# Taking four second counts of ScalarE ahead of all exponentials of a place, in a macaron attention block

## The reference

```python
q, k, v = (hidden @ W.T split into 32, 8 and 8 heads of 32)     # Wq, Wk, Wv
k, v = repeated 4 times over the heads
qr, kr = apply_rope(q, cos, sin), apply_rope(k, cos, sin)
draft = einsum('bhqd,bhkd->bhqk', qr, kr) + causal_mask
num_remain = max(min(S, 128), S - int(S * 0.9))                 # 205 of 2048
_, idx = top_k(draft, num_remain)
mask = 0 at idx, the lowest float elsewhere; the future is masked too
attn = softmax(draft_scores / sqrt(32) + mask)
out = (attn @ v) @ Wo.T
```

## Time and profile before

| | us |
|---|---|
| median of three runs | 4355.48 |
| the profiled execution, its own time | 4352.74 |
| span of its profile | 4351.0 |
| TensorE matmul busy | 3364.8 |
| VectorE busy | 3187.2 |
| ScalarE busy | 2688.8 |
| GpSimd busy | 1989.4 |

### The profile page before, as it was taken

One profiled execution on the slowest core, in us unless ns is written; L12 is line 12 of the kernel. 1 busy time (PEld: TensorE's weight loads), 2 busy tenths in 40 slices (PEclk: granted clock), 3 DMA queues, 4 the chain that ended last, 5 costly groups with the idle time before them and its releaser, 6 DMA issues. The chain is left out here.

```text
span 4351.0 us, 55631 instructions
## 1 busy us (share of the span) xinstructions
PE 3364.8 (77%) x15624; PEld 1559.5 (36%) x15864; DVE 3187.2 (73%) x6121; ACT 2688.8 (62%) x4577; POOL 1989.4 (46%) x5916
## 2 busy tenths in 40 slices
PE   7999936886787567887875678988657888886997
PEld 3444412332333233333332233333323333433444
DVE  4667657888887488888875888888568888882333
ACT  1222237887687478886875688888567888882111
POOL 1222236554356565544665455456565455572000
PEclk9999968988899689898987789999868999998998
DMA  3112120000010010001001000010010000002221
GB/s 110 62 70 71 58 57 15 9 9 9 6 23 15 20 26 10 9 9 19 13 15 31 12 12 9 7 22 12 21 28 12 9 9 9 10 17 82 77 78 44
DMA packets 221755, 123.99 MB, mean 28 GB/s; under 512 B 188164, under 2 KB 206852, under 8 KB 221316
## 3 DMA queue, kind: packets, MB, share of 16 engines
q1 hardware_dynamic: 221316, 119.36, 9.7%
HBM read 76.28 MB, written 42.99 MB: 27 GB/s over the span
## 5 line engine op out<-in xcount | busy, mean ns | idle before, releaser
L898 PE MATMUL banks<-pT,v_sb 128*65 128x512 f32 x2176 | 1182.6, 627 | 37.2 <-ACT oT L1002 35.9
L987 ACT ACTIVATE pT<-banks 128x512 f32<-128x512 f32 x1088 | 636.9, 592 | 648.0 <-PE banks L870 642.1
L846 PE MATMUL banks<-k_sb,q_sb 128*128 128x512 bf16 (+3 forms) x1188 | 475.7, 401 | 329.6 <-DVE sc L1151 295.3
L1174 DVE MAX8 near<-keys 128x8 f32<-128x256 f32 (+14 forms) x480 | 653.4, 1361 | 16.5
L978 ACT ACTIVATE junk<-sc,t_all 128x256 fp8e4<-128x256 f32 (+14 forms) x480 | 599.2, 1249 | 33.8 <-DVE sc L1151 31.9
L978 ACT ACTIVATE junk<-sc,tiny 128x256 fp8e4<-128x256 f32 (+14 forms) x480 | 595.5, 1246 | 36.4 <-DVE sc L1159 36.1
L978 ACT ACTIVATE junk<-sc,tt 128x256 fp8e4<-128x256 f32 (+14 forms) x480 | 598.5, 1247 | 2.8 <-POOL tt L1043 2.0
L848 PE MATMUL banks<-k_sb,q_sb 96*128 96x512 bf16 (+3 forms) x1280 | 502.7, 403 | 76.5 <-DVE sc L1151 70.9
L1151 DVE TENSOR_SCALAR_CACHE_REDUCE sc<-banks 128x1024 f32<-128x1024 f32 (+7 forms) x512 | 500.9, 979 | 55.6 <-PE banks L851 28.6
L1159 DVE TENSOR_SCALAR sc<-sc,tt 128x256 f32<-128x256 f32 (+14 forms) x480 | 360.6, 814 | 232.4 <-POOL tt L1064 232.2
L864 PE MATMUL banks<-q_sb,k_sb 128*128 128x512 bf16 x940 | 382.9, 407 | 131.4 <-DVE fb L1328 114.2
(11 more groups left out here) (248 smaller groups left out, 5070.1 us busy)
## 6 DMA issues: line engine op xcount, KB each, us to landing
q_sb<-scratch_qk SPq DMA_DIRECT2D x896, 32.0 KB, 1.9
scratch_qk<-parts SPq DMA_DIRECT2D x16, 960.0 KB, 3.7
a_x<-in_x SPq DMA_DIRECT2D x16, 512.0 KB, 4.2
scratch_x<-a_x SPq DMA_DIRECT2D x16, 512.0 KB, 2.9
scratch_attn<-o_sb SPq DMA_DIRECT2D x128, 64.0 KB, 1.6
c_xn<-scratch_attn SPq DMA_DIRECT2D x16, 512.0 KB, 3.7
c_x<-scratch_x SPq DMA_DIRECT2D x16, 512.0 KB, 4.6
out<-c_x SPq DMA_DIRECT2D x16, 512.0 KB, 2.6
```

Source lines behind the costliest of these rows:

```text
L846: nc.tensor.matmul(r_slot(n)[:, j:j + wj], q_sb[:, p % QS, 0, h, :], k_sb[:, group[p] % 2, 0, col:col + wj], start=True, stop=False)
L898: nc.tensor.matmul(psum[0:VP, 6, :], v_sb[:, group[p] % 2, kb, :], pT[:, n % PTS, :], start=(kb == 0), stop=(kb == blocks[p] - 1)).then_in ...
L987: nc.scalar.activation(pT[:, tn % PTS, :], psum[:, 4 + n % 2, :], ACT.Exp, scale=SCALE)\
L1174: v.max(near[:, h, :], z).then_inc(sm["key"], 1)
```

## The change

ScalarE's list of counts that come ahead of all exponentials grows from the four third counts of place j to these and the four second counts of place j + 1. The constant NARROW, compared with the number of blocks of place j + 1, is 16, and no place has more, so the condition holds in all places that are searched. What is left to spread between the exponentials is the four first counts of place j + 2.

```diff
+NARROW = TILES
...
                 for j in range(-2, N + 2):
                     counts = [(p, k, h) for p, k in ((j, 2), (j + 1, 1), (j + 2, 0)) if searching(p) for h in range(REP)]
                     first = REP if searching(j) else 0
+                    if searching(j + 1) and blocks[j + 1] <= NARROW:
+                        first += REP
                     todo = list(units[j])
```

## The result

The changed kernel takes 4393.46 us (median of four runs, 4393.13 to 4399.26); the kernel before, run beside it on the same chip, 4354.82 (four runs, 4353.22 to 4358.87). The ratio is 1.009, 95% interval 1.0073 to 1.0108: slower by 38.6 us. I predicted slower by 192, in a range of 4400 to 4700. The direction is right, the size five times too large, and the time lies 7 us under the range.

A forecast was written before the change was run, and what follows sets the result against it. No engine is full, so waits between engines set the time. Wide windows +288 and narrower ones -96 sum to +192 us on 4352.74, giving 4545, or 4547 against the median; range 4400 to 4700, 8 times in 10.

The forecast's parts named there:

- That wide places lose and narrower ones win: Phase B: the four wide windows were to lose 288 us in all, the narrower ones to gain 96.
- This loop has no slack: Widest place: ScalarE's third counts plus exponentials fill the 38.25 us, so anything put between them lengthens the place.
- it does not shrink when four counts leave it: Wide places: the stretch of exponentials is TensorE's work, busy 352.4 of 413.9 us, so moving counts out does not shorten it.
- the wide term: Wide windows: 83.8 us of moved counts less 22 of slack plus 10 for restarts, +72 each, +288 for four.
- The restart: Wide places: TensorE, after waiting before the third block, resumes at its lower clock; 10 us a window, between 0 and 20.
- Times four: Phase B: the estimate of +72 us for one wide window was taken for all four, +288.
- The narrower places: The second update comes earlier and VectorE's wait goes: 34 us gained less 10 for falling places, -24 a window, -96.
- Which wait would show it: Wide window: VectorE's wait for third counts grows about 7 us a place from 33.6; TensorE waits long for exponentials.
- my mark of 440: Wide window: if it took under 440 us, the loop was not closed as the prediction read it.
- Wide places cost nothing: Rival: VectorE's chain sets the pace everywhere and exponentials can slide; 4217 us, at the outer bound 4129; chance 0.10.
- It evens out: Rival: VectorE's waits absorb part of the delay; 24 us a wide window against 34 gained, about 4350 us; chance 0.09.
- Heavier: Rival: no slack in wide places, each with a slow restart, and narrow places limited by GpSimd; +375, 4728 us; chance 0.13.

The follow-up runs named there:

- the two halves: Second counts moved ahead only in steps of at most 10 blocks (4225.99 us), or only in steps of more than 10 (4523.34 us), each against the kernel before.
- wide_fill: wide_only plus 14 extra matmuls, their results overwritten, ahead of TensorE's second block in steps of more than 10 blocks: 4502.34 us, ratio 1.0337 against the kernel before.
- wide_only: The kernel before, with four second counts ahead of all exponentials only in steps whose running exponentials have more than 10 blocks: 4523.34 us, ratio 1.0383.

## Why the direction was right and the size wrong

**That wide places lose and narrower ones win: right.** Shown by the two halves, +166 and -132, and by their sum.

**"This loop has no slack" and "it does not shrink when four counts leave it": the step that failed.** I had put the slack at 22 us a window, between 0 and 44. In the last window it is 40: 7 of ScalarE's own idle time, and 33 by which the stretch shrinks with three counts ahead. That two counts are free shows the slack by times alone. What I had read was right where I read it: the widest place went from 38.25 to 45.28 us, as forecast, and the falling one of eleven blocks from 25.00 to 30.37. But these two were among the tightest. In the falling place of twelve blocks, one further up, the stretch gave back 4.3 of 5.4 us. I had taken TensorE's 352.4 busy us of 413.9 as proof that the stretch is full. It isn't: the 61 idle us are partly within it, and some of its work moves into the pause. This one term, 18 us too small in each of four windows, makes 72 of the 119 us by which the wide term was too large.

**The restart: right in kind, its size partly luck.** I took 10 us a window as the middle between 0 and 20, since no row showed such a pause. Under the change 34 of the 48 wide places have 512-column matmuls of 0.5 us or more within 6 us behind their first exponential, where 8 had them before; 26 restarts of 1.7 us (my figure from the earlier trace rows) would be 44 us, 11 a window, an estimate. The 20 us that `wide_fill` saved bound it from below, with 5 a window. The term for term sum of the last window of `wide_only` is 80.7 of counts (predicted 83.8) - 7 - 33 + 10 for the growth from three counts to four = +51, where +50 was measured; predicted +72. The clock gate rule of the Trainium skill ("TensorE: Matmul & The Clock Gate", Part 1), taken for every place, gave 20. The trace agrees that the lower clock comes behind a pause, and shows it in 34 places of 48 and not in all.

**Times four: wrong by the kernel's own data.** The first two wide windows were 455.4 and 434.9 us long before, not 414: in three of their places VectorE's exact fallback runs (places of 56 to 58 us), and ScalarE stands idle behind it for 15.8, 18.7 and 18.9 us. With second counts in that time it is 15.3, 19.2 and 18.7 us, so there they cost nothing. ScalarE's time between third counts and first exponential was 42.8 and 26.2 us in these windows instead of 7.3, and grew by 58.7 and 66.6 instead of 73.4. These windows cost 31 and 43, the last two 48 and 46. Four windows like the last would cost 4 x 46 = 183; the fallback places take 183 - 169 = 14 of it.

**The narrower places: right mechanism, sized too low.** I took 34 us of gain less 10 for the falling places, 24 a window. Measured: 34.9, 36.9 and 27.5 in the three whole windows, and 20.8 and 6.3 in the ten places at either end, which make up the fourth. The net loss of the falling places was 17 us over all windows (9.9 + 1.4 + 6.1) where I had 40, which is most of the difference; the gain itself, 126 + 17 = 143 us, is near my 4 x 34 = 136.

**Which wait would show it: half wrong.** I expected VectorE's wait for the third counts to grow from 33.6 by about 7 us a place. It is 33.5. The delay reached VectorE as waits for scores (from 0.4 to 40.6 us: 35.7 and 4.9) and for the flag (from 1.3 to 6.7), which together are the 45.8 us of the window. Third counts and VectorE are both later, and the wait between them keeps its size. TensorE's wait at the third block with the lower clock behind it is there as described (59.9 us, 0.61 to 0.64 us), and the wide window, 459.6, is above my mark of 440.

**The rivals.** "Wide places cost nothing" falls with `wide_only`. "It evens out" has the time within the per cent that it named (0.9%), but not by its mechanism: it had 24 us a wide window against 34, and the window costs 42 on average. "Heavier" wanted no slack at all, and one and two counts for nothing rule that out.

Not settled: how the 33 us of the stretch divide between the late first count (9 us), TensorE's work taken in the pause (16 to 17) and its idle time (8). These come from reading the traces, of which that of before lacks 34 matmuls in this window, and no kernel separates them. Nor is it settled what the slow matmuls cost: 5 us a window at least, by the estimates above 9 to 11.

## What to carry to other kernels

A closed loop read in one place holds for that place: before a moved piece of work is priced, the loop should be added up over every place of the window, with the idle time of each engine inside it. Here, with three engines each 83 to 87% busy, moved work was free at first and cost more than its length in the end, so the useful experiment is a dose (here one, two, three, four counts: -1, +1, +56, +166 us), and the useful change is a conditional one: the same edit made only where the consumer waits gave -150 us instead of +39. The same holds for a repair: head 2's scores ahead were worth 64 us with the pause of four counts, and cost 59 with that of two and 144 without.

## What the runs showed of the hardware

- The lower clock behind a new pause. Matmuls of 512 columns that took 0.5 us or more stood within 6 us behind the first exponential in 8 of the 48 wide places before, in 21 with three counts ahead (longest wait in the last window 7.9 us), in 35 with four (9.9 us) and in 34 with the whole change.
- A new pause takes only little of the lower clock away elsewhere. Between `go` and the first exponential 262 such matmuls stood before (in a trace that lacks 136 of the 512-column ones) and 239 under the change, while those behind it went from 25 to 137. With three counts it was closer to an exchange: 222 and 69.
- Matmuls without use, 168 in a window, raised the granted clock from 0.89 to 0.93 and saved 20 us of 4523 with four counts ahead. With three they raised it from 0.91 to 0.94 and cost 16 us.
